# Third and fourth layers' diagonals as four scaled copies on ScalarE, the stacks on VectorE, the low halves on GpSimd, and dispatches one transfer a step

## What is computed

```
xn = layernorm(x)
x  = x + attention_l(xn) + experts_l(xn)
# attention of layer 2 (16 heads of width 8, causal):
probs = softmax(q @ k.T * scale + causal_mask);  out = (probs @ v) @ w_out
# attention of layer 3: the same, with one rotary term shared by all heads:
scores = (q @ k.T + q_rope @ k_rope.T) / sqrt(8 + 32)
# experts: top-2, top-1, top-2 of 8; layer 3 has a shared dense expert (GELU) besides
```

## Time and profile before

| | |
|---|---|
| median of three runs | 2607.01 us |
| profiled execution, its own time | 2598.39 us |
| span of the profile | 2596.6 us |
| busy | PE 2019.9 us (78%), DVE 1908.6 (74%), ACT 1377.8 (53%), POOL 723.5 (28%) |
| DMA queues, share of 16 engines | hardware 9.8%, software 2.7% |

### The profile page before, as it was taken

How to read it: one execution, slowest core, us unless ns; L and a number is a source line. 1 busy time by engine, 2 the same in 40 slices (tenths; PEclk the granted TensorE clock), 3 DMA queues, 4 the chain that set the end, 5 groups by cost and what they waited for, 6 DMA issues and landing times.

```text
span 2596.6 us, 65873 instructions
## 1 busy us (share of the span) xinstructions
PE 2019.9 (78%) x23246; PEld 1394.1 (54%) x23247; DVE 1908.6 (74%) x4031; ACT 1377.8 (53%) x2794; POOL 723.5 (28%) x674
## 2 busy tenths in 40 slices
PE   1543679999999788815888887863899999998993
PEld 0213346666666566714555554543566666665662
DVE  2236667878788788866999998766677777776775
ACT  0231346767677655502766666430566666665552
POOL 0012685545455333323300000340720000000552
PEclk9775889999999999965988987885899998998997
DMA  8900012000000011220200000120100000000224
GB/s 226 168 0 0 26 37 72 2 3 3 3 2 2 10 48 49 61 73 15 85 2 2 2 2 5 48 64 12 51 18 2 2 2 2 2 2 10 63 62 124
DMA packets 109664, 88.07 MB, mean 34 GB/s; under 512 B 11240, under 2 KB 95816, under 8 KB 109424
## 3 DMA queue, kind: packets, MB, share of 16 engines
q1 hardware_dynamic: 97840, 60.82, 9.8%
q0 software_dynamic: 11584, 23.91, 2.7%
HBM read 45.26 MB, written 39.43 MB: 33 GB/s over the span
## 4 chain that ended last, share of the span: by engine, by line
PE 48%; DVE 28%; issue 12%; POOL 6%; ACT 3%; DMA 2%; DVEq 1%; SPq 1%; ACTq 0%; POOLq 0%
PE duo L1020 11%; PE mo L1020 10%; PE misc L1020 9%; PE acc L1020 6%; PE ob L1020 6%; DVE v L1969 4%; PE pt L1020 4%; DVE nmax L1958 3%; POOL slot_rows L623 2%; DVE nmax L2077 2%; DVE v L1802 2%; DVE nmax L1957 1%; DVE v L1794 1%; DVE region L2080 1%; DVE qT L1961 1%
## 5 line engine op out<-in xcount | busy, mean ns | idle before, releaser
L662 POOL DMA_INDIRECT results<-probT,dest_no x202 | 210.7, 1043 | 1158.5 <-ACT probT L701 1121.9
L637 POOL TENSOR_TENSOR v<-v 128x512 f16<-128x512 f32 x256 | 290.7, 1157 | 299.0 <-DVE region L2080 298.3
L1020 PE MATMUL ob<-wm,v 128*128 128x9 f16 (+1 forms) x5856 | 254.9, 180 | 72.8 <-DVE v L1969 48.9
L1020 PEld LDWEIGHTS ob<-wm,v 128*128 128x128 f16 x5856 | 222.6, 97 | 130.7 <-DVE v L1969 74.0
L903 ACT ACTIVATE v<-mo 128x384 f32<-128x384 f32 x352 | 174.2, 495 | 166.8 <-PE mo L1020 91.8
L961 ACT ACTIVATE v<-mo 128x512 f32<-128x512 f32 x256 | 153.4, 599 | 204.1 <-PE mo L1020 138.0
L1969 DVE TENSOR_TENSOR v<-v 128x768 f16<-128x768 f32 x256 | 243.5, 951 | 11.8 <-ACT v L904 11.8
L2077 DVE TENSOR_REDUCE nmax<-duo 128x2 f32<-128x512 f32 x256 | 164.8, 685 | 87.9 <-PE duo L1020 87.8
L1020 PE MATMUL duo<-kT,wm 128*128 128x256 f16 x1212 | 172.7, 279 | 55.0 <-DVE kT L1790 29.2
L1957 DVE TENSOR_REDUCE nmax<-duo 128x2 f32<-128x256 f32 x256 | 107.7, 421 | 133.6 <-PE duo L1020 132.8
L1020 PE MATMUL mo<-qT,kT 64*128 64x256 f16 (+1 forms) x2240 | 202.3, 274 | 0.0
(11 more groups left out here) (277 smaller groups left out, 4642.8 us busy)
## 6 DMA issues: line engine op xcount, KB each, us to landing
prob<-slot_rows SPq DMA_DIRECT2D x101, 130.0 KB
qT<-results SPq DMA_DIRECT2D x40, 256.0 KB, 3.1
slot_rows<-prob SPq DMA_DIRECT2D x4, 1300.0 KB, 18.6
slot_rows<-prob SPq DMA_DIRECT2D x4, 1235.0 KB, 20.1
xd<-in_L_ffn_w_dram SPq DMA_DIRECT2D x2, 2048.0 KB, 12.4
results<-probT,dest_no POOLq DMA_INDIRECT x202
slot_rows<-xd,slot_no POOLq DMA_INDIRECT x160, 2.3
x<-in_L_attn_x_dram SPq DMA_DIRECT2D x8, 256.0 KB, 4.6
```

Source lines behind the costliest of these rows:

```text
L637: pool.tensor_tensor(p16[:, p % 2, h, 1, :], p32[:, h, :], p16[:, p % 2, h, 0, :], ALU.subtract)\
L662: pool.indirect_dma_start(out=results[layer], out_offset=bass.IndirectOffsetOnAxis(ap=dest_no[:, 2 * b + t:2 * b + t + 1], axis=0), in_=y_ ...
L1020: return pe.matmul(dst, lhsT, rhs, start=start, stop=stop)
```

## The change

- Diagonals of A2 and A3: the one DVE instruction L1961 goes. ACT makes each diagonal by a copy of `small_ident` (identity / 16, 128x128, a new tile made once) with a column of `nmax4` as scale: four activations a step (`diagonals(p+2)`), behind `exps(p)` and ahead of the rest of the step.
- Stacks: 8 copies a chunk move from ACT to DVE.
- Low halves of A2 and A3: L1969 (128x768) moves from DVE to POOL.
- Dispatches: POOL sends one row tile a step, over 4 chunks in A1, 2 in A2, 4 in A3, each behind the low half of its step. POOL's A1 is unrolled.

```diff
+        small_ident = sb("small_ident", [P, P])
...
@@ -630,28 +631,30 @@   POOL, attention
-                per_step = TOP[layer] * ALL // STEPS
+                n_tiles = TOP[layer] * ALL
...
+                def pair_low(i, p):
+                    p_high.wait(pool, stage, i, 2 * p + 1)
+                    pool.tensor_tensor(p16_2[:, p % 2, 1, :], p32_2[:, p % 2, :], p16_2[:, p % 2, 0, :], ALU.subtract)\
+                        .then_inc(p_low.sem, 1)
 
-                def chunk(i, parity, more):
+                for i in range(NCH):
                     for p in range(STEPS):
-                        if p + 1 < STEPS or more:
-                            at_step(diag_made, pool, stage, i, p + 1)
-                        prob_low(i, p, 0)
-                        prob_low(i, p, 1)
-                        if isinstance(i, int) and i == 0:
-                            for n in range(per_step * p, per_step * p + per_step):
-                                send_row_tile(layer, n // ALL, n % ALL)
-
-                if layer == 1:
-                    chunks1(pool, chunk)
-                else:
-                    for n in range(per_step * STEPS):
-                        send_row_tile(layer, n // ALL, n % ALL)
+                        if layer == 1:
+                            if p + 1 < STEPS or i < NCH - 1:
+                                step1(diag_made, pool, i, p + 1)
+                            prob_low(i, p, 0)
+                            prob_low(i, p, 1)
+                        else:
+                            pair_low(i, p)
+                        n = i * STEPS + p
+                        if n < n_tiles:
+                            send_row_tile(layer, n // ALL, n % ALL)
@@ -855,11 +858,13 @@   ACT, attention (its stack and the three calls of stack in prepare go)
+                def diagonals(i, p):
+
+                    nmax_made.wait(act, stage, i, p)
+                    for n in range(4):
+                        ins = act.activation(diag2[:, p % 2, n // 2, n % 2, :], small_ident[:, :], ACT.Copy,
+                                             scale=nmax4[:, p % 2, n:n + 1])
+                    ins.then_inc(diag_made.sem, 1)
@@ -917,8 +916,10 @@
                         exps(i, p)
-                        for n in SELECT_AT.get(p, ()):
-                            stack(i, n)
+                        if p + 2 < STEPS:
+                            diagonals(i, p + 2)
+                        elif more:
+                            diagonals(i + 1, p + 2 - STEPS)
                         if layer == 3 and p in SHARED_AT:
                             shared(i, SHARED_AT[p])
@@ -930,6 +931,8 @@
+                diagonals(0, 0)
+                diagonals(0, 1)
                 chunks1(act, chunk)
@@ -1935,7 +1938,10 @@   DVE, attention
                         if p == 12:
+                            stack(i, 0)
                             keep_values(i, parity)
+                        if p == 13:
+                            stack(i, 1)
...
+                        if p == 13:
+                            stack(i, 0)
+                            stack(i, 1)
+
+                def stack(i, n):
+
+                    g, kind = n // 2, n % 2
+                    sel_full.wait(dve, stage, i, n)
+                    dve.tensor_copy((k_stack if kind else q_stack)[:, g, :], (acc if n in (0, 2) else misc)[:, :])\
+                        .then_inc(stacked.sem, 1)
@@ -1957,17 +1973,6 @@
-                    nmax_made.wait(dve, stage, i, p)
-                    dve.scalar_tensor_tensor(
-                        out=diag2[:, p % 2, :, :, :].rearrange("p q h c -> p (q h) c"),
-                        in0=ident[:, :].rearrange("p (o c) -> p o c", o=1).broadcast_to([P, 4, P]), scalar=1.0 / 16,
-                        in1=nmax4[:, p % 2, :].rearrange("p (a o) -> p a o", o=1).broadcast_to([P, 4, P]),
-                        op0=ALU.mult, op1=ALU.mult).then_inc(diag_made.sem, 1)
-
-                def pair_low(i, p):
...
@@ -1996,11 +2001,12 @@
                             maxima(i + 1, p + 2 - STEPS)
-                        pair_low(i, p)
                         if p and p % 4 == 0:
                             scale_o(i, p // 4 - 1)
                         elif p == 0 and begun:
                             scale_o(i - 1, 3)
+                        for n in SELECT_AT.get(p, ()):
+                            stack(i, n)
...
+            dve.tensor_scalar(small_ident[:, :], ident[:, :], 1.0 / 16, None, ALU.mult).then_inc(v_ones, 1)
```

More of the change, by code:

```diff
@@ L856, in attention @@
                 stage = f"A{layer}"
-                def stack(i, n):
-                    g, kind = n // 2, n % 2
-                    sel_full.wait(act, stage, i, n)
-                    copy((k_stack if kind else q_stack)[:, g, :], (acc if n in (0, 2) else misc)[:, :]).then_inc(stacked.sem, 1)
+                def diagonals(i, p):
[4 more added lines that the diff above has]
+                    ins.then_inc(diag_made.sem, 1)
                 def high(i, n, at, src, scale):
@@ L879, in prepare @@
                         if p == 12:
-                            stack(i, 0)
                             keep_values(i, parity, 2)
-                        if p == 13:
-                            stack(i, 1)
                     else:
@@ L1427, in w1_block @@
                 return lambda hl: w1[:, hl, offset + j * P:offset + (j + 1) * P]
-            pe.wait_ge(v_ones, 3)
+            pe.wait_ge(v_ones, 4)
             def turn_x1(i):
@@ L1959, in maxima @@
                         .then_inc(nmax_made.sem, 1)
-                    nmax_made.wait(dve, stage, i, p)
-                    dve.scalar_tensor_tensor(
-                        out=diag2[:, p % 2, :, :, :].rearrange("p q h c -> p (q h) c"),
-                        in0=ident[:, :].rearrange("p (o c) -> p o c", o=1).broadcast_to([P, 4, P]), scalar=1.0 / 16,
-                        in1=nmax4[:, p % 2, :].rearrange("p (a o) -> p a o", o=1).broadcast_to([P, 4, P]),
-                        op0=ALU.mult, op1=ALU.mult).then_inc(diag_made.sem, 1)
-                def pair_low(i, p):
-                    p_high.wait(dve, stage, i, 2 * p + 1)
-                    dve.tensor_tensor(p16_2[:, p % 2, 1, :], p32_2[:, p % 2, :], p16_2[:, p % 2, 0, :], ALU.subtract)\
-                        .then_inc(p_low.sem, 1)
                 def scale_o(i, g):
```

## The result

| | before | changed |
|---|---|---|
| median | 2606.23 us (4 runs, 2603.49 to 2608.66) | 2588.59 us (4 runs, 2583.97 to 2591.79) |
| profiled execution, its own time | 2598.39 us | 2591.79 us |
| ratio | | 0.9937, 95% interval 0.9922 to 0.9952 |

The kernel became 17.6 us faster, 0.63%. The forecast was 29 us faster (2578 us). Repeated beside the experiments, the changed kernel gave 2588.01 us against 2603.09, ratio 0.9942 (0.9922 to 0.9961).

A forecast was written before the change was run, and what follows sets the result against it. Limits: POOL in A1's chunk 0, DVE in A2 with PE and step latency close behind, PE in A3. Terms -46 + 10 + 6 + 1 = -29 took the median from 2607.0 to 2578 us; range 2535 to 2614.

The forecast's parts named there:

- Dispatches in A1: A1, chunk 0: sending one dispatch a step instead of four frees POOL; gain 46 us, bounds 32 and 50.
- POOL's subtraction: A2: the 768-column low half on POOL takes 1.74 us, bounds 1.3 and 1.74, 0.8 us more than DVE needs.
- ACT's copies: A2: each 128-column copy with a column operand takes 0.25 us, bounds 0.16 and 0.39; an ACT step is 2.6 us.
- the third rival: A2 and A3: ACT's copies do not overlap, 0.39 us each; together +79, 2686 us, break-even 0.29 us a copy, chance 0.05.
- A2: +10: A2: new limits cost 8 us in all, POOL's dispatches in the first two chunks +1 each; bounds -39 and +40.
- a chain of 2.60 us a step against 2.54: A2: exponentials, POOL's low half, PE's average and next scores take 5.19 us per two steps; DVE's queue stood at 2.54.
- the rival on POOL's low half: A2 and A3: POOL's longer subtraction delays averages and PE's clock falls; +40 and +24, total +19, 2626 us, chance 0.09.
- PE's waits above 6.6 us a chunk in A2 as the sign of the chain: A2: PE's waits named after POOL's subtraction exceeding 6.6 us a chunk would show the forecast wrong.
- A3: +6: A3: ACT limits steps 1 to 8, +15 us; a shorter `keep_values` wait gives -9; bounds -17 and +35.
- Two SBUF inputs: A1 and A3: DVE operations reading two SBUF operands can stretch beside POOL's subtraction, by up to 1.74 us each in A3.
- The rest: A2's end: POOL's 24 small copies move there from its head, +1 us, bounds 0 and 3; `small_ident`, made once, costs nothing.
- The relief of DVE pays: Rival, A2 and A3: PE's waits vanish in six A2 chunks (-39), A3 gains 7; -91, 2516 us, chance 0.16.

## Why the prediction was right, and where it was not

The kernel became faster, and by an amount inside the range. The size was off by 11 us, mainly by terms that were too small in A2 and in the stretch ahead of it. The term for A1 was right by its mechanism; that for A3 came close because two errors cancelled.

- *Dispatches in A1: -46.* Right. Chunk 0 gave 47.5 us, the stage 48.9, and the kernels with nothing else changed 48 to 54. Chunk 0 came out at 68.8 us, not 71.7; it is cut differently here (116.4 us before, not 119.2), and the difference of 47.5 is the same.
- *POOL's subtraction: 1.74 us.* 1.64 measured.
- *ACT's copies: 0.25 us each.* 0.295 measured, and with that a step of ACT is 1.51 + 1.18 = 2.69, not 2.6. This is past the break-even of 0.29 that the third rival named. By the prediction's own working 0.045 us more on each of 768 copies is 35 us, and the sum would have been +6 instead of -29; the kernel was faster all the same, since ACT's queue alone does not bound A2, by the estimate from the halved copies. The rival's 0.39 and its 2686 us did not come.
- *A2: +10.* The failed term: +30.7 in the pair, +24.8 in the repetition, +21 by medians. The working, a chain of 2.60 us a step against 2.54, gave +1 us a chunk, and at a like clock that is what the chunks show (0.4 to 1 us). What it left out is PE's clock: 0.82 and 0.78 granted instead of 0.90, PE busy 26 to 38 us longer on the same work. The prediction named it only in the rival on POOL's low half ("PE's clock falls behind each wait"). The rival was right that the clock would fall, and half to three quarters of its 40 us for A2 came. It was not right on the reason as far as the runs show: PE waited for the low half hardly more in sum than before (43.7 and 48.7 us against 43.4), and with the low half back on DVE the clock stayed at 0.80 and A2 at 402.9 us. What lowers the clock is open.
- *PE's waits above 6.6 us a chunk in A2 as the sign of the chain:* they were 45.2 us for POOL's low half in the stage, no more than DVE's 44.0 before. The sign looked for stayed away while the stage grew by 25 to 31 us, so it was the wrong one: the time lies in the matmuls between the waits.
- *A3: +6.* +0.9 in the pair, +4.6 in the repetition; 11 by medians. Both halves were right in kind and larger than taken: the first half grew by 3.6 us a chunk (1.9 taken; the difference is mostly the copies at 0.295 us), the second shrank by 3.7 (about 1.1 taken). That the sum came near is luck: taken times eight chunks, the errors are 14 us and 21 us and have opposite signs.
- *Two SBUF inputs.* Half of the gain at `keep_values` was held back, by the author's estimate, for stretches beside POOL's subtraction. None came there: PE's wait fell from 17.3 to 2.3 us. The reason is timing, which the prediction did not work out: of the 35 sums and differences with two SBUF inputs in A3, 28 overlap no subtraction and 7 start in the last 0.12 us of one, and none takes longer than 0.69 us. With the diagonal back on DVE the timing is another, and 14 of the 35 take 2.02 us. The stretch came above all at the diagonal, 0.69 to 1.53 us, as soon as that was put back on DVE.
- *The rest: +1, `small_ident` nothing.* The stretch between A1 and A2 cost 5 to 6 us, some 4 of them by one small operation whose code nobody edited. The stretch between A2 and A3, where the +1 was put, cost 1.6.
- *The relief of DVE pays (2516 us).* False. DVE fell from 43.6 to 26.3 us a chunk of A2 (23 taken), and no chunk came near 42.

## What to carry over

Take a change of several parts apart by stage before believing in it: here one part, the dispatches one a step, is worth 50 us, and the three moves of work around it cost 32 of them. That an engine is nearly full is no reason to move its work while other engines and the chain from step to step stand close behind; first work out the limit that takes its place. Then allow for PE's granted clock as a term of its own: here it cost more than the chain did, and neither the sum nor the length of PE's waits foretold it. A row of indirect dispatches should be spread over the steps even where a profile shows it free, since other chips paid 28 to 64 us for each.

## What the hardware showed

- Two kinds of chips: the kernel before takes 2603 to 2607 us on some and 2710 us on others. The trains of 32 and 64 indirect dispatches at the head of A2 and A3 account for some 90 of the 103 us, by the chunks of the kernels that keep them there. In the first chunk of A2, 28.6 us longer with the train than on a chip of the first kind, DVE and ACT are idle 28.5 us longer and PE 22.5, and no packet of q8 arrives within the 41 us of the train. With the dispatches spread, one kernel differs by 15 us between the kinds.
- DVE's diagonal (128x512, two SBUF inputs, 0.69 us) takes 1.53 us on average beside POOL's subtractions in A2 and 1.28 in A3; POOL's own goes from 1.64 to 1.68 us. One that starts within a subtraction ends 0.55 us behind it (114 of 116 in A2); where it keeps its 0.69 us and overlaps, POOL's takes 2.02 us.
- ACT's copy with a column as scale holds the queue 0.295 us at 128 columns and 0.24 at 64: by these two, an estimate of 0.18 us fixed.
- One 2-column DVE operation in M1 takes 0.45 us instead of 0.23 in 15 or 16 of 39 executions after edits elsewhere, about 4 us in all.
- The same 4546 matmuls of A2 keep PE busy for 332 us at a granted clock of 0.88 and 354 us at 0.82, with the same 51.5 us idle.
